# Another order of one attention period, on five engines, in a cross-attention block kernel

## The reference, cut to what matters

```
h1 = ln(x);  x = attn(h1, h1, q1, k1, v1) @ o1 + b + x
h2 = ln(x);  x = attn(h2, context, q2, k2, v2) @ o2 + b + x
h3 = ln(x);  a, g = split(h3 @ ff_w1 + b);  out = (a * gelu(g)) @ ff_w2 + b + x
attn: softmax(q k^T / 4) v, head by head
```

## Time and profile before

| | us |
|---|---|
| three runs | 1360.56, 1361.61, 1364.16 (median 1361.61) |
| profiled execution, span | 1363.1 |
| PE busy | 1311.2 |
| DVE busy | 829.1 |
| ACT busy | 678.6 |
| POOL busy | 382.2 |

### The profile page before, as it was taken

The page is one execution under the profiler, slowest core; times in us unless marked ns, Lnnn a source line. Parts: engine busy times, 40 slices in busy tenths (PEclk is TensorE's granted clock), DMA queues, the critical chain, the costliest instruction groups (busy, mean ns, idle before and its releaser), DMA issues. The chain is left out here.

```text
span 1363.1 us, 35359 instructions
## 1 busy us (share of the span) xinstructions
PE 1311.2 (96%) x13364; PEld 1217.9 (89%) x13364; DVE 829.1 (61%) x1728; ACT 678.6 (50%) x1558; POOL 382.2 (28%) x545
## 2 busy tenths in 40 slices
PE   6999789999999999999999999999889999999999
PEld 4999678898989889889899899888689999999999
DVE  5554377777777777777777777777664425252521
ACT  5664345565565565556556566556454231313131
POOL 5420312212212212212212221222166333333331
PEclk9999699999999999999999999999999999999999
DMA  4777454444454455555545444443202101010000
GB/s 126 235 254 242 133 163 140 123 142 146 119 149 134 148 148 156 156 143 152 157 132 149 128 133 136 138 125 97 69 23 73 49 2 49 0 48 0 24 1 25
DMA packets 121669, 155.60 MB, mean 114 GB/s; under 512 B 25012, under 2 KB 115372, under 8 KB 121516
## 3 DMA queue, kind: packets, MB, share of 16 engines
q1 hardware_dynamic: 121516, 153.52, 37.3%
HBM read 62.98 MB, written 28.93 MB: 67 GB/s over the span
## 5 line engine op out<-in xcount | busy, mean ns | idle before, releaser
L1362 ACT ACTIVATE probs<-expin 120x400 f32<-120x400 f32 (+2 forms) x640 | 305.0, 502 | 160.0 <-PE expin L701 151.9
L1036 DVE TENSOR_REDUCE neg_max<-score 100x2 f32<-100x722 f32 x320 | 291.3, 910 | 83.7 <-PE score L675 74.9
L701 PE MATMUL expin<-qs,ks 128*120 128x200 f32 (+2 forms) x1280 | 230.0, 278 | 6.8 <-PEq L1639 4.5
L701 PEld LDWEIGHTS expin<-qs,ks 128*120 128x120 f32 (+2 forms) x1280 | 186.9, 180 | 28.2 <-issue 10.3
L675 PE MATMUL score<-ks,qs 128*100 128x362 f32 x640 | 169.0, 345 | 5.5 <-DVE neg_max L1036 4.0
L2426 DVE SCALAR_TENSOR_TENSOR hidden<-ps_a,b_cols,gelu 128x320 f32<-128x320 f32 x100 | 55.1, 551 | 163.5 <-PE ps_a L2350 158.9
L1549 POOL TENSOR_TENSOR var_eps<-mv,eps 100x1 f32<-100x1 f32 x32 | 6.1, 189 | 418.3 <-DVE mv L1104 418.3
L2588 POOL TENSOR_TENSOR hid_lo<-hidden,hid_hi 128x320 fp32r<-128x320 f32 x100 | 89.1, 892 | 120.7 <-ACT hid_hi L2496 120.4
L2508 ACT ACTIVATE gelu<-ps_g,b_cols 128x320 f32<-128x320 f32 x100 | 52.8, 528 | 134.2 <-PE ps_g L2350 134.2
L125 DVE TENSOR_REDUCE neg_max<-score 100x10 f32<-100x1000 f32 x62 | 74.4, 1200 | 57.4 <-PE score L118 57.4
L724 PE MATMUL attn<-probs,vc 120*17 120x100 f32 (+1 forms) x3840 | 102.9, 252 | 0.1
(11 more groups left out here) (201 smaller groups left out, 2953.4 us busy)
## 6 DMA issues: line engine op xcount, KB each, us to landing
ks<-kc_parts SPq DMA_DIRECT2D x192, 181.0 KB, 2.8
qk_dram<-qk_parts SPq DMA_DIRECT2D x32, 500.0 KB, 5.5
qs<-q_parts SPq DMA_DIRECT2D x192, 75.0 KB
ks<-qk_dram SPq DMA_DIRECT2D x96, 125.0 KB
ctx_raw<-in_ctxT SPq DMA_DIRECT2D x64, 180.5 KB
ks<-kc_parts SPq DMA_DIRECT2D x96, 90.5 KB, 2.2
qs<-qk_dram SPq DMA_DIRECT2D x64, 125.0 KB
v_dram<-v_rows SPq DMA_DIRECT2D x32, 132.8 KB
```

The costliest lines, as they stand in the source:

```text
L701: mm = pe.matmul(dst, ks[a][u][:, c, j0:j0 + n], qs[a][u][:, :, q_slot(c) if a == 2 else c, :], start=True, stop=True)
L1036: ins = nc.vector.tensor_reduce(dst, src, AX_X, ALU.max, negate=True)
L1362: nc.scalar.activation(probs[e % NPT][0:n, :], expin[e % 2][0:n, 0:HG * N], ACT.Exp, scale=SCALE)\
```

## The change

The `period` functions are reordered on all five engines, and the table of `work_jobs` with them; no instruction is added or taken away, and `lead_in` and `run_out` stay as they are. In the diff, the table's rows are cut (the lines of `DRAIN_EXP` are only wrapped anew).

```diff
@@ work_jobs
-             ("O1", c, 0), ("VC", c, 0), ("T2", c, 0), ("Q2", c, 0), ("OX2", x, 0), ("OX2", x, 1), ("QT", c, 0),
+             ("VC", c, 0), ("O1", c, 0), ("VC", c, 1), ("OX2", x, 0), ("T2", c, 0), ("OX2", x, 1), ("Q2", c, 0),
...
@@ SyncE
             def period(x, s, c, f, e):
-                load_x(f)
+                place_max(1, f)
+                place_kc(c, 0)
                 load_context(f)
                 load_qkv1(e)
-                place_max(1, f)
-                place_kc(c, 0)
                 place_kc(c, 1)
                 place_q2(c)
                 place_max(2, s)
+                store_x2(x)
+                load_x(f)
                 place_kc(c, 2)
-                store_x2(x)
@@ TensorE
                 scores_for_exp(1, c, 0, 0)
+                self_scores(f, 0)
                 scores_for_exp(1, c, 1, 0)
-                self_scores(f, 0)
                 scores_for_exp(1, c, 2, 0)
+                project_kc(c, 0)
                 scores_for_exp(1, c, 3, 0)
-                project_kc(c, 0)
...
-                project_kc(c, 1)
                 times_v(1, c, 0)
...
                 times_v(1, c, 4)
+                project_kc(c, 1)
                 cross_scores(s, 0)
+                turn_outputs(1, c, 0)
                 scores_for_exp(2, x, 0, 0)
                 scores_for_exp(2, x, 0, 1)
-                turn_outputs(1, c, 0)
                 turn_outputs(1, c, 1)
...
                 scores_for_exp(2, x, 1, 1)
+                turn_max(1, f)
                 cross_scores(s, 2)
                 scores_for_exp(2, x, 1, 2)
+                turn_heads(1, c)
+                scores_for_exp(2, x, 2, 0)
                 times_v(2, x, 0)
-                scores_for_exp(2, x, 2, 0)
...
+                scores_for_exp(2, x, 4, 2)
                 times_v(2, x, 2)
...
                 cross_scores(s, 7)
+                project_vc(c, 1)
+                turn_outputs(2, x, 0)
+                turn_normalised(c)
+                cross_scores(s, 8)
+                turn_outputs(2, x, 1)
                 project_q2(c)
-                turn_outputs(2, x, 0)
-                turn_outputs(2, x, 1)
-                turn_q2(c)
-                cross_scores(s, 8)
-                project_vc(c, 1)
                 turn_heads(2, x)
                 project_vc(c, 2)
+                turn_q2(c)
                 cross_scores(s, 9)
@@ ScalarE
                 exponential(2, x, 2, 0)
+                max_high(1, f)
+                heads_high(1, c)
                 exponential(2, x, 2, 1)
-                heads_high(1, c)
-                max_high(1, f)
...
@@ VectorE
                 maximum(2, s, 9)
+                result(x)
                 max_low(2, s)
-                result(x)
+                q2_low(c)
...
@@ GpSimd
                 inverse_deviation(c)
+                split_context(f)
+                first_residual(f)
                 second_residual(c)
-                first_residual(f)
-                split_context(f)
```

More of the change, by code:

```diff
@@ L44, in work_jobs @@
     order = [("KC", c, 0), ("KC", c, 1), ("OX1", c, 0), ("OX1", c, 1), ("KC", c, 2), ("MT1", f, 0), ("OT1", c, 0),
-             ("O1", c, 0), ("VC", c, 0), ("T2", c, 0), ("Q2", c, 0), ("OX2", x, 0), ("OX2", x, 1), ("QT", c, 0),
-             ("VC", c, 1), ("OT2", x, 0), ("VC", c, 2), ("O2", x, 0), ("MT2", s, 0)]
+             ("VC", c, 0), ("O1", c, 0), ("VC", c, 1), ("OX2", x, 0), ("T2", c, 0), ("OX2", x, 1), ("Q2", c, 0),
+             ("OT2", x, 0), ("VC", c, 2), ("QT", c, 0), ("O2", x, 0), ("MT2", s, 0)]
     return [job for job in order if job[1] is not None]
@@ L151 @@
                (2, 31, 6), (2, 31, 7), (2, 31, 8), (2, 31, 9)]
-DRAIN_EXP = [(1, 31, 0, 0), (1, 31, 1, 0), (1, 31, 2, 0), (1, 31, 3, 0), (1, 31, 4, 0), (2, 29, 0, 0), (2, 29, 0, 1),
[7 rows of a table removed]
+DRAIN_EXP = [(1, 31, 0, 0), (1, 31, 1, 0), (1, 31, 2, 0), (1, 31, 3, 0), (1, 31, 4, 0), (2, 29, 0, 0),
[8 rows of a table added]
 DRAIN_PV = [(1, 31, 0), (1, 31, 1), (1, 31, 2), (1, 31, 3), (1, 31, 4), (2, 29, 0), (2, 29, 1), (2, 29, 2),
@@ L965, in period @@
                 times_v(1, c, 4)
+                project_kc(c, 1)
                 cross_scores(s, 0)
+                turn_outputs(1, c, 0)
                 scores_for_exp(2, x, 0, 0)
                 scores_for_exp(2, x, 0, 1)
-                turn_outputs(1, c, 0)
                 turn_outputs(1, c, 1)
+                cross_scores(s, 1)
                 scores_for_exp(2, x, 0, 2)
-                cross_scores(s, 1)
                 scores_for_exp(2, x, 1, 0)
@@ L975, in period @@
                 scores_for_exp(2, x, 1, 1)
+                turn_max(1, f)
                 cross_scores(s, 2)
                 scores_for_exp(2, x, 1, 2)
+                turn_heads(1, c)
+                scores_for_exp(2, x, 2, 0)
                 times_v(2, x, 0)
-                scores_for_exp(2, x, 2, 0)
                 cross_scores(s, 3)
                 scores_for_exp(2, x, 2, 1)
-                turn_max(1, f)
-                turn_heads(1, c)
                 scores_for_exp(2, x, 2, 2)
+                times_v(2, x, 1)
                 scores_for_exp(2, x, 3, 0)
                 cross_scores(s, 4)
-                project_out(1, c)
                 scores_for_exp(2, x, 3, 1)
+                project_vc(c, 0)
                 scores_for_exp(2, x, 3, 2)
-                project_vc(c, 0)
                 scores_for_exp(2, x, 4, 0)
                 cross_scores(s, 5)
+                project_out(1, c)
                 scores_for_exp(2, x, 4, 1)
-                times_v(2, x, 1)
+                cross_scores(s, 6)
+                scores_for_exp(2, x, 4, 2)
                 times_v(2, x, 2)
-                scores_for_exp(2, x, 4, 2)
-                cross_scores(s, 6)
-                turn_normalised(c)
                 times_v(2, x, 3)
@@ L1258, in period @@
                 kc_low(c, 0)
+                maximum(2, s, 0)
                 kc_low(c, 1)
-                maximum(2, s, 0)
                 divide(1, c, 0)
@@ L1265, in period @@
                 kc_low(c, 2)
+                max_low(1, f)
                 maximum(2, s, 3)
                 features_low("OT1", c)
-                max_low(1, f)
                 maximum(2, s, 4)
+                maximum(2, s, 5)
                 second_input(c)
-                maximum(2, s, 5)
+                maximum(2, s, 6)
                 normalise(c)
-                maximum(2, s, 6)
-                features_low("T2", c)
                 maximum(2, s, 7)
                 divide(2, x, 0)
+                features_low("T2", c)
                 divide(2, x, 1)
-                q2_low(c)
                 maximum(2, s, 8)
@@ L1500, in period @@
                 exponential(1, c, 3, 0)
+                kc_high(c, 0)
                 exponential(1, c, 4, 0)
-                kc_high(c, 0)
+                copy_product(1, c)
                 kc_high(c, 1)
-                copy_product(1, c)
                 exponential(2, x, 0, 0)
@@ L1522, in period @@
                 exponential(2, x, 4, 2)
+                copy_product(2, x)
+                copy_vc(c, 0)
+                copy_vc(c, 1)
                 features_high("T2", c)
-                copy_vc(c, 0)
-                copy_product(2, x)
                 copy_q2(c)
+                heads_high(2, x)
                 q2_high(c)
-                copy_vc(c, 1)
-                heads_high(2, x)
                 copy_vc(c, 2)
```

## The result

| | us |
|---|---|
| before, median of 4 runs | 1362.9 (1360.6 to 1364.2) |
| after, median of 4 runs | 1380.9 (1379.5 to 1382.5) |
| ratio, 95% interval | 1.0131 (1.0115 to 1.0147) |

The changed kernel is 1.3% slower, by 18 us. The forecast was + 29 us, 1391, in 1364 to 1412; it started from the 1361.6 us of the first three runs of the kernel before, and the fourth moved that median to 1362.9.

The account below looks back on a forecast made before the run. SyncE's queue was to bound the changed kernel: ring 18.5 + 1.75 + 3.8 + 1.55 = 25.6 us, with 1.3 of stalls 26.85 a period, + 1.0 over 29 periods, + 29 us: 1391 us, range 1364 to 1412.

Parts of the forecast that it names:

- The ring: From SyncE's self maxima through cross maxima, PE and ScalarE back to SyncE: 25.6 us, 26.85 per period with stalled issues; chance 0.63.
- SyncE's leg: SyncE's issues from the start of `place_max(1, f)` to the end of `place_max(2, s)`: 18.5 us without a stalled issue.
- stalled ones: SyncE's issues that take longer than bare ones: 1.5 us per period, 1.3 of it put on the ring's path.
- Issues are cheap when they come late: Rival: SyncE's spread order has no stalled issues, so the ring hides behind PE; 1356 us, chance 0.10.
- Landing, PE and ScalarE: The ring's other terms: maxima landing to the matmul 1.75 us, PE between exponential groups 3.8, `max_high(1, f)` behind its exponential 1.55.
- PE alone: PE's period in the new order without SyncE's limit: 25.84 - 1.1 + 0.34 + 0.6 = 25.65 us.
- The stalls: PE's waits in the old order, about 1.1 us a period, all taken as gone.
- The short new ones: New short stalls on PE in the new order, some 0.6 us a period.
- the steps from turn to float32r: On PE, a float32r group after a float32 turn costs 0.08 to 0.09 us more; nine instead of five: + 0.34.
- GpSimd costs nothing: On GpSimd, the context's split still begins at the end of `project_vc(c, 2)`, so its new order adds no time.
- the self stacks land late: Rival: `load_qkv1` lands late for the next period's `self_scores(f, 0)`; 27.6 us a period, 1412 us, chance 0.17.
- The signs: Expected profile: SyncE waiting 3 to 4 us before self maxima, PE 0.5 to 1.5 at L702, records 26.8 apart.

## Why the forecast was right

**The bound and its mechanism** were right. The ring from `place_max(1, f)` over `place_max(2, s)` and `scores_for_exp(2, x, 0, 0)` back to the self maxima sets the period. Taking DMAs out of it shortens the period until the next ring stops it, a DMA put into it lengthens it by more than its issue, and one put beside it costs nothing.

**SyncE's leg**: 18.5 us of bare issues and 1.3 of stalled ones, 19.8. Measured 19.75 on average. Of it 7.4 us in the window, 0.26 a period, are waits in front of keys and queries and not issues, which the sum didn't have; so the stalled issues are some 1.0 and not 1.3, and that the leg came out to 0.05 is in part luck. *Issues are cheap when they come late* is refuted; L442 still has a most of 1666 ns (before 2067).

**Landing, PE and ScalarE**: 1.75 + 3.8 + 1.55 = 7.1 us forecast, 1.37 + 3.60 + 1.44 = 6.4 measured, 6.69 on average. The landing of the maxima, for which no view of before had a row, was the largest part of the miss. Forecast ring 26.85, measured 26.39; the 0.46 are nearly all here. That is why + 29 us became + 18: 29 x 0.46 is 13, which leaves 16 us in the periods, and the medians differ by 18.

**PE alone**: 25.65 forecast, 25.42 measured with SyncE out of the way. The stalls were taken away, as assumed. The short new ones and the steps from turn to float32r came to less than 0.34 + 0.6, or the old ones to more than 1.1; no run separates these. The forecast time didn't use the term, since SyncE's ring was the longer.

**What was missed.** The forecast knew two rings, that of the cross maxima and, as a rival, that of the self stacks. There are two more: the queries' (26.02 us with SyncE's old order), whose turn I had looked at only for PE's own wait at `turn_q2`, and the context's, which has some 1.5 us of slack here and closes when the stacks go first. "GpSimd costs nothing" held, as forecast: the split follows `project_vc(c, 2)` by 0.45 us, as before. Had the queries' ring been on paper, the forecast would have read that PE's new order can't win even under SyncE's old one: 25.84 before, 25.42 for PE's order, 26.02 with the queries' ring, 26.39 with SyncE's order.

**The signs.** The wait before the self maxima is 3.2 us a period (3 to 4 forecast), the one before `place_q2` almost nil, PE's share 95%: right. PE's wait for the maxima is at most 13.6 us in 28.42 periods, 0.48, just under the 0.5 to 1.5 named, and it comes in 14 of them, not in most; `turn_q2` waits 0.13 where under 0.1 was named. The records stand 26.4 apart, not 26.8. The wait at L118 is larger than forecast for this case, and was named as the mark of *the self stacks land late*; as a mark it was a bad one, since it shows a ring's slack and not its length. The run with the keys later decided against that rival.

**The rule on issue time.** The Trainium skill, "DMA: Bandwidth & Descriptors", section "Issuing engines are not separate DMA queues", takes the sequencer's time to initiate a DMA as usually small relative to the DMA itself. For one DMA the trace agrees: 0.47 us of issue for the added one, 2.0 to landing. That this time can be left out of account here, the runs contradict: the same DMA cost 0.81 us a period inside the ring, and nothing outside.

## What to carry to other kernels

A queue that only issues DMAs is an engine with a busy time of its own (23 of 26 us here), and a wait put at its head makes everything behind it part of a ring with whoever is waited for. Before moving a wait forward, write down each ring that passes through the queue, and sum it: issues, landing, and the work from the reader back to the writer. A wait in the profile tells which ring has no slack at that moment; which one sets the period is told by adding or removing an issue in one of them alone.

## What was not expected of the hardware

- The same DMAs come to a little less time of issue in the new order, 22.95 us a period instead of 23.3. What makes a single issue long (up to 1.7 us at L442 here) no run shows.
- With the stacks first, the context's data, issued with other DMAs before and behind it, was read 6.1 to 7.2 us after the end of its issue, where the keys of the changed kernel land in 2.1 to 4.9 us from the start of theirs, and the maxima are read 1.4 us after the end of theirs. What makes the difference wasn't tried.
- A wait that a row puts down to a DMA can be one for PE: GpSimd's for the context in the changed kernel, which ended 0.45 us behind the same matmul whether the context's issue had ended 7, 9 or 14 us before (the changed kernel, with the keys later, with the context first).
- After 5.5 us without work PE came back at a granted clock of 0.50, and the five matmuls of the first projection were 0.30 us apart, against 0.18 in the changed kernel (426.71 to 426.89).
